# Perceiver block on one core: the first layer norm by halves inside the cross-attention's block, and the first loads in another order

## The reference

```
x = x + xattn(layernorm(x), ctx, ctx)      # the change is here
x = x + mamba(layernorm(x))
x = x + ffn(layernorm(x))
x = x + xattn16heads(layernorm(x), ctx, ctx)
x = x + attn(layernorm(x))
x = x + experts(layernorm(x))

layernorm(x) = (x - mean) / sqrt(var + 1e-5)
xattn(x, c, c):  q = x Wq + bq;  k = c Wk + bk;  v = c Wv + bv
                 softmax(q k^T / 16) v
```

## Time and profile before

| what | value |
|---|---|
| median of 3 runs | 772.3 us |
| the profiled execution | 772.14 us |
| its span, first to last instruction | 770.4 us |
| PE busy | 676.5 us, 88% |
| DVE busy | 492.2 us, 64% |
| ACT busy | 374.3 us, 49% |
| mean granted clock of TensorE | 0.953 of full speed |

### The profile page before, as it was taken

The page is one execution under the profiler, slowest core; times in us unless marked ns, Lnnn a source line. Parts: engine busy times, 40 slices in busy tenths (PEclk is TensorE's granted clock), DMA queues, the critical chain, the costliest instruction groups (busy, mean ns, idle before and its releaser), DMA issues. The chain is left out here.

```text
span 770.4 us, 10238 instructions
## 1 busy us (share of the span) xinstructions
PE 676.5 (88%) x3718; PEld 457.3 (59%) x3718; DVE 492.2 (64%) x775; ACT 374.3 (49%) x719; POOL 242.8 (32%) x167
## 2 busy tenths in 40 slices
PE   2999999989929988989888999986986959899998
PEld 2445555543326555655556888854554545699897
DVE  3223343458569989889894357899874665555455
ACT  2221111235498988889883333334672442544342
POOL 1000000000059998979770000456830130220000
PEclk9999999999969999999999999998997979799999
DMA  9989999818202332222200000000001120100000
GB/s 349 347 340 414 422 422 377 309 62 213 85 27 86 106 107 86 93 83 99 83 29 1 0 15 15 0 16 16 1 1 55 56 54 1 46 10 1 27 1 29
DMA packets 31046, 86.39 MB, mean 112 GB/s; under 512 B 7882, under 2 KB 19556, under 8 KB 28820
## 3 DMA queue, kind: packets, MB, share of 16 engines
q1 hardware_dynamic: 29892, 84.75, 30.4%
q10 hardware_dynamic: 1104, 0.98, 0.4%
HBM read 83.50 MB, written 1.11 MB: 110 GB/s over the span
## 5 line engine op out<-in xcount | busy, mean ns | idle before, releaser
L677 POOL TENSOR_TENSOR dbu<-du,bs 128x1024 f32<-128x1024 f32 x64 | 150.6, 2369 | 233.3 <-DVE du L867 215.4
L968 PE MATMUL Y<-weighed,ident 128*128 128x512 f32 (+1 forms) x256 | 101.3, 517 | 0.0
L877 DVE TENSOR_TENSOR_SCAN w_in<-A,dbu 128x1024 f32<-128x1024 f32 x42 | 95.2, 2276 | 0.1
L770 ACT ACTIVATE weighed<-T,CT 128x256 f32<-128x256 f32 x208 | 83.0, 472 | 22.5 <-PE T L958 20.0
L759 ACT ACTIVATE A<-delta,negA 128x504 f32<-128x504 f32 x128 | 83.0, 692 | 1.7 <-DVE xn L877 1.7
L968 PEld LDWEIGHTS Y<-weighed,ident 128*128 128x128 f32 x256 | 43.9, 192 | 29.8 <-issue 29.2
L958 PE MATMUL T<-ident,w_in 128*128 128x128 f32 x336 | 45.3, 279 | 12.3 <-ACT weighed L770 7.3
L958 PEld LDWEIGHTS T<-ident,w_in 128*128 128x128 f32 x336 | 37.4, 142 | 28.3 <-DVE w_in L877 14.8
L877 DVE TENSOR_TENSOR_SCAN xn<-A,dbu 128x1024 f32<-128x1024 f32 x22 | 50.1, 2278 | 1.0 <-issue 1.0
L312 PE MATMUL O<-cN,pT 128*64 128x256 f32 x384 | 46.7, 385 | 0.0
L300 PE MATMUL S<-cT,qkT 128*64 128x512 f32 (+1 forms) x256 | 45.6, 509 | 0.0
(11 more groups left out here) (340 smaller groups left out, 1385.3 us busy)
## 6 DMA issues: line engine op xcount, KB each, us to landing
cT<-in_ctxT SPq DMA_DIRECT2D x8, 3202.0 KB, 13.7
cN<-in_ctx SPq DMA_DIRECT2D x8, 3072.0 KB, 12.7
bs<-b_rows SPq DMA_DIRECT2D x32, 512.0 KB, 3.7
raw_w<-in_w SPq DMA_DIRECT2D x16, 256.0 KB, 3.1
w<-in_w SPq DMA_DIRECT2D x7, 256.0 KB, 8.2
vs<-vx SPq DMA_DIRECT2D x8, 136.0 KB, 2.4
x<-in_x SPq DMA_DIRECT2D x1, 1024.0 KB, 6.0
cR<-in_ctx SPq DMA_DIRECT2D x1, 1024.0 KB, 21.4
```

The source lines that it names most:

```text
L677: e.tensor_tensor(dbu[s % NB][:, :, :], half(m.du, s // DS), row, ALU.mult).then_inc(s_bu, 1)
L770: i = e.activation(weighed[s % 2][:, q * Q:(q + 1) * Q], T[:, q * Q:(q + 1) * Q], ACT.Copy, scale=c_of(s, q))
L877: e.tensor_tensor_scan(S[s % NS], A[s % 2][:, :], dbu[s % NB][:, :, :].rearrange("p c n -> p (c n)"), 0.0, ALU.mult, ALU.add).then_inc(s_h, 1)
L968: e.matmul(Y[:, w], k.ident[:, :], weighed[s % 2][:, w], start=False, stop=True, skip_group_check=True).then_inc(s_y, 1)
```

## The change

- The block `layer_norm` is gone, and one barrier with it. Its work is in `cross_attention`, in two halves of four tiles: DVE normalises a half into `prob[half]` (buffers of the softmax, which are free then); PE turns it over into the banks of `S` (`turn_first`); ACT has `root_first` and `move_first`, which moves a bank of two tiles at a time.
- `x` is loaded by two DMAs with a semaphore each. `wq0` and `wk0T` are asked for on SP's queue, behind `x` and ahead of `cT`. ACT's queue has `cols`, the row `bv0`, and `wv0`, which has a semaphore of its own, `k.s_wv`, and is waited for in `project_out(0)`.
- `s_w0` is complete at 48 (`cols`, `wq0`, `wk0T`).

```diff
-layer_norm(nc, k, "ln0")                      # the function and its call
+++ cross_attention, tensor
-            e.wait_ge(k.s_w0, k.n_w0)
+            e.wait_ge(k.s_const, k.n_ident)
+            def turn_first(half):
+                for t in range(4 * half, 4 * half + 4):
+                    e.wait_ge(s_x0, t + 1)
+                    for c in range(KD):
+                        i = e.transpose(bank[t // 2][:, (2 * (t % 2) + c) * P:(2 * (t % 2) + c + 1) * P],
+                                        prob[half][:, (t % 4) * D + c * P:(t % 4) * D + (c + 1) * P], k.ident[:, :])
+                    if t % 2:
+                        i.then_inc(s_t0, 1)
             def project(half):
+                e.wait_ge(s_e0, 2 * half + 2)
...
             def project_out(i):
                 e.wait_ge(s_oe, i + 1)
+                if i == 0:
+                    e.wait_ge(k.s_wv, 16)
...
+            turn_first(0)
+            e.wait_ge(k.s_w0, k.n_w0)
             project(0)
+            turn_first(1)
             e.wait_ge(s_pe, 4)
+            e.wait_ge(s_e0, 4)
             scores(0)
             project(1)
+++ cross_attention, scalar
+            def root_first(half):
+                e.wait_ge(s_n0, 4 * half + 3)
+                e.activation(sd[:, 4 * half:4 * half + 4], veps[:, 4 * half:4 * half + 4], ACT.Sqrt).then_inc(s_r0, 1)
+            def move_first(n):
+                e.wait_ge(s_t0, n + 1)
+                e.activation(k.xT[:, :, 2 * n * P:(2 * n + 2) * P].rearrange("p c (u n) -> p c u n", u=2),
+                             bank[n].rearrange("p (u c n) -> p c u n", u=2, c=KD), ACT.Copy).then_inc(s_e0, 1)
+            root_first(0)
+            root_first(1)
+            move_first(0)
+            move_first(1)
+            e.wait_ge(k.s_w0, k.n_w0)
             move(0)
+            move_first(2)
+            move_first(3)
             softmax(0)
+++ cross_attention, vector
+            for half in range(2):
+                ts = range(4 * half, 4 * half + 4)
+                hs = slice(ts[0], ts[-1] + 1)
+                e.wait_ge(k.s_x[half], 16)
+                for t in ts:
+                    j = tile_stats(e, k, t)
...
+                e.tensor_scalar(veps[:, hs], mv[:, hs, 1], EPS, None, ALU.add).then_inc(s_n0, 1)
+                e.wait_ge(s_r0, half + 1)
+                e.reciprocal(rstd[:, hs], sd[:, hs]).then_inc(s_n0, 1)
...
+                    e.tensor_scalar(prob[half][:, (t % 4) * D:(t % 4 + 1) * D], k.x[:, t, :], mv[:, t, 0:1], rstd[:, t:t + 1],
+                                    ALU.subtract, ALU.mult).then_inc(s_x0, 1)
+++ perceiver, sync and scalar
-                e.dma_start(k.x[:, :, :], t["x"].rearrange("b l d -> (b l) d").rearrange("(t p) d -> p t d", p=P)
-                            ).then_inc(k.s_x, 16)
+                for half in range(2):
+                    ts = slice(4 * half, 4 * half + 4)
+                    e.dma_start(k.x[:, ts, :], tiles[:, ts, :]).then_inc(k.s_x[half], 16)
+                for n, w in (("wq0", k.wq0), ("wk0T", k.wk0T)):
+                    e.dma_start(w[:, :, :], t[n].rearrange("(c p) n -> p c n", p=P)).then_inc(k.s_w0, 16)
                 for i in range(2):
                     load_columns(e, k, i, i)
...
                 e.dma_start(k.cols[:, :], t["cols"]).then_inc(k.s_w0, 16)
-                for n, w in (("wq0", k.wq0), ("wk0T", k.wk0T), ("wv0", k.wv0)):
-                    e.dma_start(w[:, :, :], t[n].rearrange("(c p) n -> p c n", p=P)).then_inc(k.s_w0, 16)
                 load_vectors(e, 0, 1, k.s_bv)
+                e.dma_start(k.wv0[:, :, :], t["wv0"].rearrange("(c p) n -> p c n", p=P)).then_inc(k.s_wv, 16)
```

More of the change, by code:

```diff
@@ L76, in rowvec @@
     return k.rows[:, ROWV[name], :]
[L79 to L139, removed]
@@ L227, in cross_attention @@
         rstd = sb("a_rstd", [P, TILES])
+        s_n0 = sem("a_n0")
+        s_r0 = sem("a_r0")
+        s_x0 = sem("a_x0")
+        s_t0 = sem("a_t0")
+        s_e0 = sem("a_e0")
         s_st = sem("a_st")
@@ L440, in _ @@
         def _(e):
+            for half in range(2):
[4 more added lines that the diff above has]
+                    j = tile_stats(e, k, t)
+                j.then_inc(s_n0, 1)
+                e.wait_ge(s_n0, 4 * half + 1)
+                for t in ts:
+                    j = e.bn_aggr(mv[:, t, :], k.stats[:, t, :])
+                j.then_inc(s_n0, 1)
+                e.wait_ge(s_n0, 4 * half + 2)
+                e.tensor_scalar(veps[:, hs], mv[:, hs, 1], EPS, None, ALU.add).then_inc(s_n0, 1)
+                e.wait_ge(s_r0, half + 1)
+                e.reciprocal(rstd[:, hs], sd[:, hs]).then_inc(s_n0, 1)
+                e.wait_ge(s_n0, 4 * half + 4)
+                for t in ts:
+                    e.tensor_scalar(prob[half][:, (t % 4) * D:(t % 4 + 1) * D], k.x[:, t, :], mv[:, t, 0:1], rstd[:, t:t + 1],
+                                    ALU.subtract, ALU.mult).then_inc(s_x0, 1)
             e.wait_ge(k.s_bv, 16)
+            e.wait_ge(s_x0, TILES)
             e.tensor_tensor(k.x[:, :, :], k.x[:, :, :],
@@ L2546, in perceiver @@
         k.s_bv = sem("s_bv")
-        k.s_x, k.s_rows, k.s_const, k.s_w0 = (sem(n) for n in ("s_x", "s_rows", "s_const", "s_w0"))
+        k.s_rows, k.s_const, k.s_w0, k.s_wv = (sem(n) for n in ("s_rows", "s_const", "s_w0", "s_wv"))
+        k.s_x = [sem(f"s_x{i}") for i in range(2)]
         k.n_ident = k.n_const = 8 + 3 + 3 + E
-        k.n_w0 = 64
+        k.n_w0 = 48
         k.w_in = sb("w_in", [P, KD, 2 * DI])
@@ L2588, in _ @@
             def _(e):
-                e.dma_start(k.x[:, :, :], t["x"].rearrange("b l d -> (b l) d").rearrange("(t p) d -> p t d", p=P)
-                            ).then_inc(k.s_x, 16)
+                tiles = t["x"].rearrange("b l d -> (b l) d").rearrange("(t p) d -> p t d", p=P)
+                for half in range(2):
[3 more added lines that the diff above has]
+                    e.dma_start(w[:, :, :], t[n].rearrange("(c p) n -> p c n", p=P)).then_inc(k.s_w0, 16)
                 for i in range(2):
```

## The result

The changed kernel takes 767.96 us at the median of 20 runs (765.60 to 770.51), the kernel before 772.5 us at the median of 20 (767.52 to 776.91). The ratio is 0.9931, with a 95% interval of 0.9908 to 0.9955: 4.5 us less, clear of noise. The 20 times of the kernel before lie in three groups: 4 at 767.5 to 768.8, 7 at 771.75 to 772.52 and 9 at 776.2 to 776.9; the changed kernel has none above 770.51. The profiled execution took 765.64 us, its span is 763.9.

A forecast was written before the change was run, and what follows sets the result against it. TensorE was taken to bound the kernel, setting the loop's pace. Earlier `project(0)` -3.8, slower first products +0.8 and new path work +2.0 gave -1.0 us: forecast 771.2 us, range 768.0 to 774.0.

The forecast's parts named there:

- The start of `project(0)` after the change: Ahead of the loop: `project(0)` starts at 14.1, the moves waiting on ACT behind the second half's root.
- The first products: First eight records of `project(0)`: 6.2 us instead of 5.40, between 3.7 and 7.0 by clock level, adding 0.8 us.
- the new work on the path: Between the one-column products and `scores(0)`: the second half's transposes and moves add 2.0 us; `scores(0)` starts at 28.4.
- The start that it is compared with: In the kernel before, `project(0)` starts at 17.90, released by the landing of `wv` after a 2.74 us standstill.
- -3.8 (start of `project(0)`): Term of the sum ahead of the loop: `project(0)` starts at 14.1 instead of 17.90, 3.8 us earlier.
- the load is late: Rival at the front: `x` halves land late, each microsecond past 6.64 costing one; 772.5 us, chance 0.05.
- The sum: Whole kernel: -3.8 + 0.8 + 2.0 = -1.0 us, giving 771.1 for the profiled execution and 771.2 for the median.
- A low `scores(0)`: Rival at the loop's start: `scores(0)` at the low clock level costs 1.7 us; 773.2 to 774.1, chance 0.20.
- The low stretch at 46: After the one-column products, the clock falls by 46 to 47; a rival with chance 0.08 had it gone, worth 1.7.
- more than the sum: Rival: high clock throughout at the front and low stretch at 46 gone, 5.2 us gained; 767.1, chance 0.08.
- The page's rule: At the front: if transposes do not raise the clock, `scores(0)` begins low and the sum is +0.7, not -1.0.
- The loop: Cross-attention loop: TensorE sets the 15.05 us period, `cT` has 24.5 us and needs at most 23.0, so gains stay.

The follow-up runs named there:

- e12: The kernel before, unchanged, traced in another execution: 772.39 us.
- e5: The kernel before with one edit, a semaphore of its own for `wv0`, loads keeping their queues and order: median 767.33 us, ratio 0.9932.
- e2: The changed kernel with the loads of the kernel before (`x` in one transfer, all weights on ACT's queue and one semaphore): median 773.54 us, ratio 1.0002.
- e8: The changed kernel with ACT's second root behind the first moves and the second half's transposes between products of `project(0)`: median 764.16 us, ratio 0.9899.
- e9: e8 with twelve unread transposes of the identity on TensorE ahead of the first half's own: median 767.78 us, ratio 0.9951.
- e11: e8 with both the twelve extra transposes of e9 and the 64-column products of e10: median 766.94 us, ratio 0.9926.
- e3: The changed kernel with ACT's second square root moved behind the first half's two moves: median 767.04 us, ratio 0.9927.
- e10: e8 with the one-column products made 64 columns wide: median 765.69 us, ratio 0.9907.
- e6: The kernel before with the first transfer on SP's queue (`x`) held back until GpSimd's second constant: median 769.57 us, ratio 0.9959.
- e1: The kernel before with the new order of loads alone, the norm staying in its block: median 767.47 us, ratio 0.9935.
- e7: The kernel before with the first transfer on ACT's queue (`cols`) held back until GpSimd's second constant: median 776.59 us, ratio 1.0058.

## Why the prediction was wrong

- **The start of `project(0)` after the change, and what delays it.** Right: 13.88 for 14.1, ACT's second root in front of the moves.
- **The first products, and the new work on the path.** Right: 6.15 for 6.2; 1.8 us between the one-column products and `scores(0)` for 2.0; `scores(0)` at 27.91 for 28.4. The gain between the two profiles, 1.5 us, is in the forecast's own range.
- **The start that it is compared with.** This step failed. I took "-3.8 (start of `project(0)`)" from 17.90, one landing of one transfer in one execution, and set the sum against a median over executions. The runs showed the landing at 17.9 or at 20.9 to 21.0 with the same loads (with the very same program, 17.90 in the first trace and 20.93 in e12). With the late one the term is 7.0 to 7.1 and the gain at `scores(0)` is 5.1 us (33.04 to 27.91). The median's 4.5 us lies between 1.5 and 5.1, and clock differences are mixed in. That the wait is what the gain comes from is shown by e5, which takes only the value weights out of it and gains 4.9 us, and by e2, which has the new norm with the old wait and gains nothing.
- **What was behind it.** I read the standstill as one of 2.74 us with a named cause, and did not ask how firm the cause was. The spread of the three runs, 768.76 to 772.45, I put down to the clock alone. The removal of a variable wait was the change's main effect, and none of my rivals had it; "the load is late" looked at the new loads and not at the old ones.
- **The sum.** It is off by tenths, which decides nothing: 772.3 less 1.0 is 771.3 and not 771.2, and eight steps at the low level with their end are 7.1 rather than 7.0, since 3.70 is 0.3 longer than eight high steps. The profiled execution came out 5.5 us below the 771.1 forecast for it: 0.5 us are path, and 5.0 us are low stretches that the first profile has and this one has not (1.5 us at 46, 3.5 us behind the loop). No run shows that the change removed them, so this part of that pair is luck.
- **The rivals.** A low `scores(0)` did not come. The low stretch at 46 did go, in the profiled pair: this part of "more than the sum" happened, but e5 and e8 have such a stretch again at 42, so it is not the change's merit.
- **The page's rule.** The Trainium skill, "TensorE: Matmul & The Clock Gate", Part 4 (PE-mode transpose), says that the high level does not engage for transposes. The fp32 transposes here contradict it twice more: e9 and e11 had twenty transposes ahead of `project(0)` and then 3.67 us for its first eight records, where e3, e8 and e10, with eight transposes and the same 0.78 us of standstill, had 6.26, 6.45 and 5.80. How many are enough the runs do not say: after sixteen transposes and 0.73 us e5 and e6 had 3.67, and e1 had 5.74.
- **The loop.** Right that it passes the gain on, within the gain of this change. Wrong in how much reserve it has: I compared the steady wait for a `cT`, 24.5 us, with its longest landing, 23.0, and took from it that what is won stays won; e9, with `scores(0)` 6.3 us earlier than the changed kernel, ran into a limit at the third `cT`, which landed 26.3 us after its issue.

What stays open: how often the kernel before has the late front (three of the five profiles with its loads, one of the two of the kernel itself), and how much of the 4.5 us is due to low stretches in later stages. e1 and e6 have `scores(0)` within 0.03 us of each other and medians 2.1 us apart, on two chips, so that part is not small. The fourteen traces give its size. From the first product of the next layer to the end they took 602.3 to 602.4 us in two (the changed kernel, e3), 603.6 to 604.2 in seven, and 605.8 to 606.3 in five (before, e5, e7, e8, e10). The granted clock tells these apart: the first two have no low stretch near 420 or 720 us, the seven have one near 420, the five have both. It does not go by the version of the kernel alone: the kernel before is among the five with its first trace and among the seven with e12. With the 3.7 us between the two fronts of the kernel before (29.38 and 33.04) and the 1.5 of a low `scores(1)`, this adds up to 8.9 us, an estimate beside the 9.4 us that its 20 times spread. What decides where a low stretch falls was not tested.

## What to carry to other kernels

A wait in one profile has the length of that execution. If what ends it is a transfer that competes with another queue from the first microsecond, look at several executions, and at what the wait does not need: here one semaphore for a tensor that is used 50 us later gave as much as the whole rewrite. And a front can be shortened only until the transfers behind it become the bound; past that point the wait comes back later, and in the two traces in which it came back with more than 4 us (e9, e11) TensorE ran at the low level after it.

## What the runs showed of the hardware

- Two queues that start at the same time share the engines differently from one execution to the next: `cols`, 62 KB, landed 2.4 us after its issue in one and 3.9 in the other, and everything behind it on ACT's queue moved by the same 3 us or so. Held back by 0.8 us on one side or the other, the value weights landed 13.5 or 20.1 us after their issue.
- Beside the transfers of `cT` ACT's queue is slow: in the kernel before and in e12 its 256 KB weights landed 4.5 to 4.9 us apart, near 57 GB/s of the 420 or so in all. The Trainium skill, "DMA: Bandwidth & Descriptors" (Queues, rings and completion order), says that each engine takes the queues by turns, packet by packet. With as many rows in a packet of either queue, rows of 1 KB against rows of 6.4 KB, that would be one part in 7.4, an estimate of 57 GB/s from the tensors' rows. These two traces agree. In e6, whose ACT queue was served first, the last two weights landed 7.5 us apart (8.2 and 15.7), which this estimate does not give.
- The clock column shows 1.00 until the first change is recorded, also where every step is at the low level (steps of 0.85 us under a 1.00 in 15 to 16 us of the changed kernel).
